# A two-layer model in one kernel: later stages joined to one pipeline by batch, gates inside the recurrence, a deeper scatter ring

## What is computed

```python
# layer 0, attention: 16 heads of 8, a delta-like recurrence over the batch's rows; then
x = x + _L0_attn_ref(_layernorm(x), Wq, Wk, Wv, Wbeta, Wg, Wout, ln_g, ln_b)
# layer 0, experts: 8 experts, top 2, at most 512 tokens each
x = x + _L0_ffn_ref(_layernorm(x), rw1, rb1, rw2, rb2, ew1, eb1, ew2, eb2)
# layer 1, attention (gated linear attention), h = _ln(x, ln_w, ln_b), x already a layernorm
gk = jax.nn.log_sigmoid(h @ gk_w1 @ gk_w2 + gk_b2) / GATE_NORM
def step(S, inp):
    qt, kt, vt, gt = inp
    S = jnp.exp(gt)[..., None] * S + kt[..., None] * vt[..., None, :]
    return (S, jnp.einsum('bhk,bhkv->bhv', qt, S))
o = _rms(o, rms_w) * (g * jax.nn.sigmoid(g))
x = x + o.reshape(Bb, Tt, HEADS * DV) @ Wo
h2 = _ln(x, ln_w, ln_b)
x = x + jax.nn.gelu(h2 @ W1 + b1, approximate=False) @ W2 + b2
# layer 1, experts: softmax over 16, top 4, every expert applied to every token
logits = hidden_states @ router_w + router_b
out = sum_e (gelu(x @ w1e + b1e) @ w2e + b2e) * ce
```

## Time and profile before

| | |
|---|---|
| median of 3 runs | 1094.68 us (1094.51 to 1095.32) |
| the profiled execution | 1097.08 us, its span 1095.2 us |
| TensorE clock granted, mean | 0.901 |
| busy share PE, DVE, ACT, POOL | 78%, 55%, 55%, 55% |

### The profile page before, as it was taken

How to read it: one execution, slowest core, us unless ns; L and a number is a source line. 1 busy time by engine, 2 the same in 40 slices (tenths; PEclk the granted TensorE clock), 3 DMA queues, 4 the chain that set the end, 5 groups by cost and what they waited for, 6 DMA issues and landing times.

```text
span 1095.2 us, 17990 instructions
## 1 busy us (share of the span) xinstructions
PE 856.1 (78%) x5763; PEld 504.7 (46%) x5763; DVE 597.7 (55%) x1650; ACT 599.8 (55%) x877; POOL 602.6 (55%) x384
## 2 busy tenths in 40 slices
PE   2963555679993498288299658777999999999998
PEld 1321112144441376022133235665777777777776
DVE  4429999945762011473388396774444444444444
ACT  1642333324441143276544206557989889889896
POOL 4005999530667245100288307515877777777776
PEclk9986899888997699598699888868999999999999
DMA  4799000053000300500500000000000000000000
GB/s 121 111 117 244 0 0 1 0 122 109 31 12 6 80 17 18 165 0 1 154 1 0 0 1 1 1 0 1 12 0 10 0 10 10 0 10 10 0 11 11
DMA packets 49901, 38.24 MB, mean 35 GB/s; under 512 B 5259, under 2 KB 41854, under 8 KB 49854
## 3 DMA queue, kind: packets, MB, share of 16 engines
q1 hardware_dynamic: 46782, 35.17, 14.2%
q0 software_dynamic: 3072, 2.51, 0.8%
HBM read 18.05 MB, written 14.88 MB: 30 GB/s over the span
## 4 chain that ended last, share of the span: by engine, by line
PE 37%; DVE 7%; POOL 4%; ACT 3%; issue 1%; DVEq 0%; POOLq 0%; ACTq 0%
PE PS L1375 36%; POOL scratch L537 2%; DVE scratch L1081 1%; PE PS L1382 1%; DVE scratch L976 1%; POOL A L611 1%; ACT scratch L851 1%; DVE stats L958 1%; DVE scratch L1273 0%; POOL resid L607 0%; POOL resid L606 0%; DVE A L1095 0%; DVE scratch L1336 0%; DVE scratch L1270 0%; PE PS L1732 0%
## 5 line engine op out<-in xcount | busy, mean ns | idle before, releaser
L618 POOL TENSOR_TENSOR scratch<-scratch 128x1024 f16<-128x1024 f32 x128 | 273.0, 2132 | 115.2 <-ACT scratch L943 114.9
L1360 DVE SCALAR_TENSOR_TENSOR resid<-PS,coef,resid 128x128 f32 x512 | 144.7, 344 | 197.2 <-PE PS L1375 196.4
L1375 PEld LDWEIGHTS PS<-A,scratch 128*128 128x128 f16 (+1 forms) x3328 | 211.8, 105 | 30.9 <-issue 1.3
L1375 PE MATMUL PS<-A,scratch 128*128 128x128 f16 (+1 forms) x3328 | 222.3, 224 | 0.2
L1375 PE MATMUL PS<-A 128*128 (+1 forms) x768 | 189.5, 384 | 11.3 <-ACT scratch L939 11.3
L939 ACT ACTIVATE scratch<-PS,cols 128x512 f32<-128x512 f32 x256 | 167.8, 685 | 26.7 <-PE PS L1375 25.8
L1375 PE MATMUL PS<-scratch,ident 128*128 128x512 f32 x176 | 100.0, 694 | 71.9 <-DVE scratch L1059 58.3
L943 ACT ACTIVATE scratch<-scratch 128x1024 f16<-128x1024 f32 x128 | 135.3, 1057 | 5.3
L505 POOL TENSOR_TENSOR scratch<-A 128x1024 f32<-128x1024 f32 x32 | 76.9, 2423 | 90.1 <-DVE A L1034 75.5
L1375 PEld LDWEIGHTS PS<-A 128*128 128x128 f16 x768 | 70.6, 99 | 76.1 <-ACT scratch L939 11.7
L1375 PEld LDWEIGHTS PS<-scratch,ident 128*128 128x128 f32 x176 | 32.9, 210 | 133.0 <-DVE scratch L1059 87.5
(11 more groups left out here) (256 smaller groups left out, 1215.7 us busy)
## 6 DMA issues: line engine op xcount, KB each, us to landing
A<-A SPq DMA_DIRECT2D x24, 256.0 KB, 5.5
y_rows<-zeros SPq DMA_DIRECT2D x8, 512.0 KB, 6.0
A<-y_rows SPq DMA_DIRECT2D x16, 256.0 KB, 3.6
disp<-zeros SPq DMA_DIRECT2D x4, 528.0 KB, 18.8
A<-disp SPq DMA_DIRECT2D x4, 528.0 KB, 5.9
resid<-in_L_attn_x SPq DMA_DIRECT2D x8, 256.0 KB, 4.7
A<-scratch SPq DMA_DIRECT2D x8, 256.0 KB, 4.4
A<-in_L_ffn_ew SPq DMA_DIRECT2D x1, 2048.0 KB, 12.2
```

The lines of the kernel that those rows point to most:

```text
L618: pool.tensor_tensor(h_low[n % 4], h_full[n % 2], h_high[n % 4], SUB).then_inc(S("m1_low"), 1)
L1360: last = STT(out=resid[:, g, :], in0=bank(4 + e % 2)[:, t * C:(t + 1) * C], scalar=coef1[:, g, e:e + 1], in1=resid[:, g, :], op0=MUL, op1=ADD)
L1375: return nc.tensor.matmul(o, l, r, start=start, stop=stop)
```

## The change

**Layer-0 output and scatter (stage 5).** RING5 is 7. Project_bias, copy_p2 and add_p2 of batches 4 to 7 move into the loop, count_picks and place_picks stand earlier in it, s_scattered is two semaphores (batch 0, the others). **Stage 6.** The bias addition, its semaphore and the outputs' matmul groups are by tile, 32 instead of 8.

**Stage 7.** u_gk = gk_w1 @ gk_w2 is made once at the start of stage 3 (a transpose, a matmul, two copies) and the g1 projection goes. Combine is 3 batches ahead, not 2; hT_copy and the transposes stand earlier. **Gates** go by two batches on 512 columns: gates(0) after batch 6 in stage 7, gates(1) to gates(3) after the two key copies of batches 0 to 2 in the recurrence. Stage ends 7, 8, 10 and 11 go. **Recurrence.** Loops are unrolled; GpSimd's write_c is two steps ahead of its pair_sum; outputs go to one bank with the square at once (outputs), the head sums stand in TensorE's order, and Silu in ScalarE's from batch 4 on. **Stages 10 to 12** become one loop by batch with statistics and roots by batch; GpSimd scales the weights once at its start. The expert weights are loaded when the last combine is done. x_hl, w1_hl, w2_hl, eb2_rep and some scratch buffers have new places; some semaphores are shared under new names.

```diff
+        P2_BANK = (1, 2, 1, 2, 4, 4, 4, 4)
...
-        STAGES = (0, 1, 3, 5, 6, 7, 8, 9, 10, 11, 12)
+        PAIRS = DK // 2
+        STAGES = (0, 1, 3, 5, 6, 9)
...
-        RING5 = 4
+        RING5 = 7
...
-            sp.wait_ge(stage_done, ended(7))
+            sp.wait_ge(S("moe_added"), at(B - 1))
...
-                for b in range(B):
-                    for p in range(pairs):
-                        n = layer[0] + b * pairs + p
-                        pool.wait_ge(S("r_coef"), at(n))
-                        pool.wait_ge(S("r_scanned"), at(n, 2))
-                        pool.tensor_tensor(cbuf[p % 2], cs[p % 2],
-                                           v[:, bts(b, T)].unsqueeze(1).to_broadcast([128, 2, T]),
-                                           MUL).then_inc(S("r_c"), 1)
-                        if n > layer[0]:
-                            pair_sum(n - 1)
-                pair_sum(layer[0] + B * pairs - 1)
...
+            for b in range(B // 2):
                 add_p2(b)
-                if b < RING5:
-                    write_ids(b)
+            for b in range(RING5):
+                write_ids(b)
             pool.wait_ge(s_zeroed, 16 * ((ROWS + YROWS) // 1024))
             for b in range(B):
+                if b + B // 2 < B:
+                    add_p2(b + B // 2)
                 scatter(b)
-                if b + RING5 < B:
-                    write_ids(b + RING5)
+                if b == RING5 - 4:
+                    write_ids(B - 1)
...
+            def write_c(n):
+                b = n // PAIRS
+                pool.wait_ge(S("r_coef"), at(n))
+                pool.wait_ge(S("r_scanned"), at(n, 2))
+                pool.tensor_tensor(cbuf[n % 2], cs[n % 2], v1[:, bts(b, T)].unsqueeze(1).to_broadcast([128, 2, T]),
+                                   MUL).then_inc(S("r_c"), 1)
+
+            def pair_sum(n):
+                pool.wait_ge(S("r_prod"), at(n))
+                pool.tensor_tensor(prod[n % 2][:, 0, :], prod[n % 2][:, 0, :], prod[n % 2][:, 1, :],
+                                   ADD).then_inc(S("r_pair"), 1)
+
+            pool.wait_ge(S("kq_low"), at(B - 1))
+            write_c(0)
+            write_c(1)
+            for n in range(B * PAIRS):
+                if n + 2 < B * PAIRS:
+                    write_c(n + 2)
+                pair_sum(n)
             stage_end(pool, 9)
...
+            def gates(m):
+                c = bts(m, T)
+                act.wait_ge(S("gate_low"), at(m, 1))
+                st.done(A_(ga, gate[:, c], ACT.Abs))
+                st.done(A_(gb, ga, ACT.Exp, scale=-1.0))
+                A_(ga, gb, ACT.Ln, bias=1.0).then_inc(S("gate_ln"), 1)
+                act.wait_ge(S("gate_log"), at(m))
+                st.done(A_(gate[:, c], gb, ACT.Exp, scale=1.0 / GATE_NORM))
+                A_(gate_hl[:, 0, c], gate[:, c], ACT.Copy).then_inc(S("gate_high"), 1)
...
+                if b == B - 2:
+                    gates(0)
...
+            def outputs(b):
+                act.wait_ge(S("r_acc"), at(b * PAIRS + PAIRS - 1))
+                act.wait_ge(S("rms_mm"), at(b, 2))
+                A_(o1[:, bts(b, T)], bank(6), ACT.Copy)
+                A_(sq[b % 2], bank(6), ACT.Square).then_inc(S("o1_sq"), 1)
+
+            def silu(b):
+                A_(sg1[:, bts(b, T)], sg1[:, bts(b, T)], ACT.Silu).then_inc(S("sg_silu"), 1)
+
+            for b in range(B):
+                for p in range(PAIRS):
+                    keys(b * PAIRS + p)
+                if b:
+                    outputs(b - 1)
+                if b < B // 2 - 1:
+                    gates(b + 1)
+                if b >= B // 2:
+                    silu(2 * (b - B // 2))
+                    silu(2 * (b - B // 2) + 1)
+            outputs(B - 1)
+            act.wait_ge(S("rms_mm"), at(B - 1))
+            A_(nrm[:, 0:512], bank(7), ACT.Sqrt, scale=1.0 / D, bias=epsc[:, 0:1]).then_inc(s_nrm, 1)
             stage_end(act, 9)
...
+            deviation11(0)
+            hT11_copy(0)
+            for b in range(B):
+                gelu11(b)
+                if b + 1 < B:
+                    deviation11(b + 1)
+                if b:
+                    xs_copy(b - 1)
+                if b == 0:
+                    act.wait_ge(s_scaled, 2)
+                weights_high(b)
+                if b + 1 < B:
+                    hT11_copy(b + 1)
+                deviation12(b)
+            xs_copy(B - 1)
...
-            for e in range(E0):
-                dve.wait_ge(S("m0_out_mm"), at(e))
-                TT(eo[:, bts(e, NT), :], bank(6 + e % 2).rearrange("p (n c) -> p n c", c=C),
-                   eb2_rep[:, e, :].unsqueeze(1).to_broadcast([128, NT, C]), ADD).then_inc(S("eo"), 1)
+            for n in range(E0 * NT):
+                dve.wait_ge(S("m0_out_mm"), at(n))
+                TT(eo[:, n, :], bank(6 + n % 2)[:, 0:C], eb2_rep[:, n // NT, :], ADD).then_inc(S("eo"), 1)
...
+                if b == B - 1:
+                    gates(0)
+                    gates_low(0)
+                kq_low(b, b % 2)
+                if b + 3 < B:
+                    combine(b + 3)
                 if b + 2 < B:
-                    combine(b + 2)
-                if b + 1 < B:
-                    make_z(b + 1)
-                kq_low(b, b % 2)
-            stage_end(dve, 7)
-
-
-            st.done(TS(gm, gate, 0.0, None, ALU.min))
-            dve.wait_ge(s_ln_high, 1)
-            TT(gb, gm, ga, SUB).then_inc(s_log, 1)
-            dve.wait_ge(s_ln_high, 2)
-            TT(gate_hl[:, 1, :], gate, gate_hl[:, 0, :], SUB)
-            stage_end(dve, 8)
-
-
-            with dve.Fori(0, B) as b:
-                for p in range(DK // 2):
-                    n = b * (DK // 2) + (LAYER1[0] + p)
-                    dve.wait_ge(S("r1_e"), at(b * (DK // 2) + p))
-                    scan(LAYER1, n, p, bank(2, 2))
-                    read_out(LAYER1, n, p)
+                    make_z(b + 2)
...
+            for b in range(B):
+                for p in range(PAIRS):
+                    scan(b * PAIRS + p)
+                    read_out(b * PAIRS + p)
+                if b < B // 2 - 1:
+                    gates(b + 1)
+                    gates_low(b + 1)
+            dve.wait_ge(s_nrm, 3)
+            st.done(V.reciprocal(rn[:, 0:512], nrm[:, 0:512]))
...
+            dve.wait_ge(S("sg_silu"), at(B - 1))
+            gate_y(0)
+            add_z(0)
+            gate_y(1)
+            normalise11(0)
+            for b in range(B):
+                if b:
+                    normalise12(b - 1)
+                if b + 1 < B:
+                    add_z(b + 1)
+                if b + 2 < B:
+                    gate_y(b + 2)
+                if b + 1 < B:
+                    normalise11(b + 1)
+                if b:
+                    split_x(b - 1)
+                add_mlp(b)
+                if b:
+                    add_logits(b - 1)
+            normalise12(B - 1)
+            split_x(B - 1)
+            add_logits(B - 1)
...
-            project_bias(4)
-            project_bias(5)
-            project_bias(6)
-            project_bias(7)
-            pe.wait_ge(S("p2_copied"), at(B - 1))
+            pe.wait_ge(S("p2_copied"), at(B // 2 - 1))
             transpose5(0)
             for b in range(B):
+                if b == 0:
+                    router_hidden(b)
                 if b + 1 < B:
                     project0(b + 1)
-                router_hidden(b)
+                if b:
+                    count_picks(b - 1, (b - 1) % 2)
+                    router_hidden(b)
                 if b + 2 < B:
                     centre(b + 2)
-                if b:
-                    count_picks(b - 1, (b - 1) % 2)
                 router_logits_T(b)
+                if b + B // 2 < B:
+                    project_bias(b + B // 2)
                 if b + 1 < B:
                     transpose5(b + 1)
                 router_logits(b)
...
+            def keys(n):
+                pe.wait_ge(S("r_coef"), at(n, 1))
+                picked_pair(0, lambda j: pickg[:, 0, 2 * (n % PAIRS) + j, :], kq_hl, n // PAIRS).then_inc(S("r1_k"), 1)
+
+            def decays(n):
+                b = n // PAIRS
+                pe.wait_ge(S("gate_low"), at(b // 2))
+                pe.wait_ge(S("r_scanned"), at(n, 1))
+                picked_pair(2, lambda j: pickg[:, b % 2, 2 * (n % PAIRS) + j, :], gate_hl, b // 2).then_inc(S("r1_e"), 1)
+
+            def queries(n):
+                pe.wait_ge(S("r_prod"), at(n, 1))
+                picked_pair(4, lambda j: pickg[:, 1, 2 * (n % PAIRS) + j, :], kq_hl, n // PAIRS).then_inc(S("r_q"), 1)
+
+            def sum_up(n):
+                b, p = n // PAIRS, n % PAIRS
+                pe.wait_ge(S("r_pair"), at(n))
+                if p == 0:
+                    pe.wait_ge(S("o1_sq"), at(b, 1))
+                mm(bank(6), ident[:, :], prod[n % 2][:, 0, :], start=p == 0, stop=p == PAIRS - 1).then_inc(S("r_acc"), 1)
+
+            def head_squares(b):
```

(39 more changed lines are left out.)

562 lines of the change are left out of this document (248 added, 314 removed), and 3 rows, old and new, of the table SIGNALS.

## The result

The changed kernel takes 1164.17 us (median of 4 runs, 1163.3 to 1165.42), the kernel before 1094.74 in the same comparison: 1.0634 times as long, 95% interval 1.0616 to 1.0653. Slower was forecast, 1133 and at most 1160; it is slower by 69.4 where 38 were forecast, and 4 us beyond the upper end of the range. The profiled execution has a span of 1162.3, 67.1 over the span before.

The account below looks back on a forecast made before the run. Before the layer-1 experts no engine was full except in the recurrences; waits between engines bound much of the rest. Terms 1.2 - 6.4 - 3.1 - 21.2 + 70.0 - 2.1 = +38.4 on 1095.2 gave 1133 us median, range 1112 to 1160.

Parts of the forecast that it names:

- The ring: Layer-1 recurrence: GpSimd's product two ahead puts TensorE, ScalarE and GpSimd in series, 7.9 us a step instead of 4.09.
- Recurrence and norms: Layer-1 recurrence and its norms: 88.9 us before, 158.9 after, +70.0, with ends 145 and 172.
- TensorE's part of a step, 2.84, at a granted clock of 0.9: Layer-1 recurrence: the lower clock adds 0.32 us to a step, 4.4 over 14 steps.
- rival (b): Layer-1 recurrence: the clock falls in longer steps, 1.4 to 2.8 more each, +30 to +45, 1168 us; chance 0.07.
- Stage 5: Layer-0 scatters: seven buffers remove four waits of 2.3 us; TensorE then bounds, with 0.95 for projection, 0.3 for count; -6.4.
- the gap that I took as gone: Stage 6: 2.21 us before the last eight scatters, said to vanish with additions by tile; stage forecast -3.1.
- Stages 7 and 8: To the first recurrence matmul: shorter rounds, no stage 8, no rank-16 round trip, less gates moved forward; -21.2 us.
- The pipeline: Stages 10 to 12 as one loop by batch: VectorE bounds at 9.4 us a batch, 97 in all, -2.1.
- 1.2 a batch: Joined pipeline: time given back for GpSimd work lying beside VectorE's, 9.6 us over eight batches.
- Rival (c): Joined pipeline loses: normalisations 5 us instead of 1.1 in most batches, or ScalarE bounds; +14, 1147 us; chance 0.08.
- Rival (a): Layer-1 recurrence: the product and its copy always stand ready, step stays at 4.1 us, 1071 in all; chance 0.10.
- Rival (d): Nothing nets out: recurrence step about 5.4 us, cancelled by gains of stages 5 to 8; 1095 us; chance 0.03.

Follow-up runs that it names:

- e1: The changed kernel with GpSimd's order of before in the layer-1 recurrence (product one step ahead of the pair sum, not two): 1082.69 us, ratio 0.9872.
- e2: The kernel before with one edit: GpSimd's pair sum of step n-2 instead of n-1 behind the product of step n: 1179.76 us, ratio 1.0764.
- e3: The changed kernel with twelve unused matmuls in each recurrence step, while TensorE waits for the pair sum: 1145.4 us, ratio 1.0444.
- e8: e1 with ScalarE's gates of batches 2 to 7 cut into three parts and VectorE's gate steps spread over different steps: 1076.39 us, ratio 0.9799.
- e6: e1 with stage 5's orders as in the kernel before, keeping only the ring of seven buffers: 1082.34 us, ratio 0.9873.
- e5: e1 with two more GpSimd waits in the joined pipeline, keeping its work off VectorE's normalisations: 1071.7 us, ratio 0.9776.
- e9: e5 with Relu in place of Gelu in the joined pipeline, which takes away 16 table loads: 1072.52 us, ratio 0.9791.
- e4: The changed kernel with Relu in place of Gelu in the joined pipeline, which takes away 16 table loads: 1178.79 us, ratio 1.0746.

## Why the prediction was wrong, step by step

**The sign and the cause were right, the size was not.** The ring was named with its members and its place, and e1 and e2 show it from both sides: undone it gives 81, alone it costs 84. The steps below failed in size.

**Recurrence and norms, +85.0 for +70.0: the clock.** The step at fault is "TensorE's part of a step, 2.84, at a granted clock of 0.9", put at 4.4 us with support from the layer-0 recurrence, busy 55% at 1.00. The clock was 0.76, and e3 takes back 17.6 of it, so this term alone misses by 13 or more of the 15. The comparison with layer 0 did not hold. TensorE was busy 55% here too (96.3 of 174.0), but partly because of the lower clock: the same 241 matmuls take 75.0 in e1. And in the layer-0 recurrence TensorE pauses only 1.6 us between pieces of 2.0 (timeline of the kernel before; the last row is a stretch of it, in the form of the earlier trace rows):

```profile
123.89 1.98 PE L1375 MATMUL PS<-scratch,ident 128*128 128x512 f32 x4 [1.57 <-DVE scratch L1059]
127.44 1.98 PE L1375 MATMUL PS<-scratch,ident 128*128 128x512 f32 x4 [1.57 <-DVE scratch L1059]
```

```profile
160.00:165.00 5.00, 3.44 (x5) 1.10 (x6) 4.82 (x6) 1.81 (x3) 5.00 (x3) 0.68 0.00 0
```

Here it pauses 3.9 in each step. The last row shows that 1.00 was not kept all through layer 0 either: right behind the earlier trace rows's 40 us the clock is 0.68. What makes it fall is not isolated by any run. That was rival (b), given 0.07; it was not a rival to the ring but its consequence (in e1 the clock is 0.88). Its condition came true, about half the time at 1.2 GHz, its price of 30 to 45 did not: the low end of its own 1.4 to 2.8 a step, 20 over 14 steps, is near the 17.6. With the clock at 0.89 the sum of steps holds to 2 us. Within it, a gate stall was put at 5.0 each: steps with a gate take 13.7 and 13.9 from sum_up to sum_up against 9.4 without, 4.3 each (below, the second row to the third has a gate between); e8 takes back 9.8 for the three with their clock.

```profile
533.46 2.08 PE L1422 MATMUL PS<-scratch,ident 128*128 128x512 f32 x2 [9.07 <-POOL scratch L590]
...
542.90 1.13 PE L1422 MATMUL PS<-scratch,ident 128*128 128x512 f32 x2 [3.89 <-POOL scratch L590]
...
556.61 2.07 PE L1422 MATMUL PS<-scratch,ident 128*128 128x512 f32 x2 [8.30 <-POOL scratch L590]
```

**Stage 5, +0.3 for -6.4.** Two terms failed. The waits for a buffer were taken as loss, 2.3 each, but the scatters had gone at 11.5 a batch (274.22 to 354.7 for seven) and TensorE's batch is 11.3: with them gone the slots are late instead, and e6 gains 4.6 from first to last scatter. And "0.95 for the projection and 0.3 for the earlier count" was 1.0 and 0.56: the count (L1422 with tri) waits 0.16 to 0.49 for picked and its matmuls stand in the open, so TensorE's batch is 12.6 to 12.9 with a projection and 11.9 without. The scatters came 13.2 to 13.4 apart in the first batches, and the last batch's began at 355.52, where its slots had been put at 347.9; TensorE's batch explains only part of that, the rest is open.

**Stage 6, -1.8 for -3.1.** The failed term is the gap that I took as gone; it is still there, as long as in the earlier trace rows, only one microsecond earlier. What the last scatters wait for behind VectorE's addition was not tested:

```profile
432.02 0.97 POOL L574 DMA_INDIRECT y_rows<-A  x1 [2.21 <-DVE A L1192]
```

**Stages 7 and 8, -22.3 for -21.2.** Right. A round of kq_low in the changed kernel, as computed, takes 6.95 and 6.80 where the earlier trace rows had 7.28:

```profile
483.70 0.69 DVE L1224 TENSOR_TENSOR A<-PS,A 128x512 f16<-128x512 f32 x1 [1.26 <-ACT A L814]
...
490.65 0.69 DVE L1224 TENSOR_TENSOR A<-PS,A 128x512 f16<-128x512 f32 x1 [1.41 <-ACT A L814]
...
497.45 0.69 DVE L1224 TENSOR_TENSOR A<-PS,A 128x512 f16<-128x512 f32 x1 [1.26 <-ACT A L814]
```

**The pipeline, +4.4 for -2.1.** The work and its bound were right once GpSimd was kept away: e5 and e9 show VectorE as the bound of the middle batches at 8.8 each and the loads hidden to 1.4 us. The failed term is the give-back of "1.2 a batch" for GpSimd: it was 1.9 in the changed kernel (32.8 - 17.9, over eight), which is 5.3 of the 6.5, and 3.1 in e4, 0.1 in e5. It is not a mean to be carried over from the stages before; it depends on which VectorE instruction GpSimd's work happens to meet, and a batch loop repeats the meeting. Rival (c) had 5 us for a normalisation in most batches; in the changed kernel one of a batch's two takes 2.8 to 3.1 in six batches and 4.7 in one. The Trainium skill, "ScalarE: Activation LUTs", section "What ACT_TABLE_LOAD costs", has a drain behind each load; nothing shows of it here either: in e9 sixteen loads cost 1.4 us together, and rows of loads still read 1.28 with the function 1.30 after the start.

**Rival (a)** is refuted for this order; with the order of before (e1) the loop does run at 4.3 a step. **Rival (d)** has no support.

## What to carry to other kernels

Moving a producer further ahead on an in-order engine moves everything behind it later: before a queue is reordered, follow each ring through all engines' queues once and count how many steps it spans; a ring that spanned two steps and now spans one makes each step a whole round trip, here 9 to 10 us for 4.3, and can be seen on paper. Where such a ring leaves a matmul engine idle for several microseconds a step, price its own part at the lower clock too, as the far end of the range. And where two engines disturb each other, two waits that keep their work apart can be worth more than any instruction saved.

## What the runs showed of the hardware

TensorE's granted clock was 0.76 in a loop in which it stood idle for about 3.9 us in nearly each step of 9 to 11, 0.68 in e2 with the same pauses in 10.3, and 0.88 in e1, where only three waits are long (2.7 to 3.4); 12 matmuls with unused results in each pause brought it from 0.76 to 0.89 and the kernel's time down by 18.8 us. Four of VectorE's TENSOR_SCALAR on float32 tiles of 128x128 take 1.11 when GpSimd is kept away (e5) and 4.97 beside four GpSimd operations of 4.8 together (e4), 1.19 to 1.42 each. The statistics and an addition that reads PSUM keep the times that they have elsewhere (0.87 for four, 0.69): in the changed kernel the addition lies within GpSimd's scaling of the weights (third row), and so does most of the statistics.

```profile
693.92 0.69 DVE L1301 TENSOR_TENSOR A<-A,PS 128x512 f32<-128x512 f32 x1 [2.17 <-PE PS L1422]
694.64 0.87 DVE L1292 BATCH_NORM_STATS2 stats<-A 128x6 f32<-128x128 f32 x4
```

```profile
691.30 3.92 POOL L605 TENSOR_SCALAR A<-A 128x4096 f32<-128x4096 f32 x1
```

The Trainium skill, "SBUF — State Buffer", section "SBUF: two separate sides", describes a pair of ports that VectorE, in some of its modes, and GpSimd take for a whole instruction, while the other stands. The rows agree: in e4 each of the four takes about as long as one GpSimd operation (1.1 to 1.3).
